# Expert stage of a mixture-of-experts block: another order of casts, token turns and comparisons

## What is computed

```
scores = softmax(xf @ router_w + router_b)
G, idx = top_k(scores.T, 512)                # 8 experts, 512 tokens each
toks = xf[idx]
h1 = relu(einsum('ekh,ehf->ekf', toks, w1) + b1)      # 256 -> 1024
eo = einsum('ekf,efh->ekh', h1, w2) + b2              # 1024 -> 256
y = zeros_like(xf).at[idx].add(eo * G)
x = x + gb * y
```

## Time and profile before

| | us |
|---|---|
| median of 3 runs | 1748.44 (1747.86 to 1748.75) |
| the profiled execution's own time | 1750.26 |
| its span in the profile | 1748.4 |
| PE busy in the span | 1678.7 |
| DVE busy | 1516.8 |
| ACT busy | 1286.0 |
| POOL busy | 232.6 |

### The profile page before, as it was taken

The page is one execution under the profiler, slowest core; times in us unless marked ns, Lnnn a source line. Parts: engine busy times, 40 slices in busy tenths (PEclk is TensorE's granted clock), DMA queues, the critical chain, the costliest instruction groups (busy, mean ns, idle before and its releaser), DMA issues. The chain is left out here.

```text
span 1748.4 us, 42933 instructions
## 1 busy us (share of the span) xinstructions
PE 1678.7 (96%) x16853; PEld 949.0 (54%) x16853; DVE 1516.8 (87%) x1956; ACT 1286.0 (74%) x2425; POOL 232.6 (13%) x300
## 2 busy tenths in 40 slices
PE   7999999999999999999999999999999997499997
PEld 4645555555555555555555555555555585277776
DVE  5578999999999999999999999999999386677873
ACT  2326888888888888888888888888888824266561
POOL 0422012100010000001000000100000012134453
PEclk9999999999999999999999999999999995599999
DMA  8660343222222233223222223332220332244532
GB/s 276 190 175 26 88 102 51 42 41 39 53 53 39 40 53 52 42 41 64 42 39 39 41 53 52 60 48 40 42 39 12 109 116 60 85 109 104 138 67 30
DMA packets 95719, 121.99 MB, mean 70 GB/s; under 512 B 26124, under 2 KB 72780, under 8 KB 92412
## 3 DMA queue, kind: packets, MB, share of 16 engines
q1 hardware_dynamic: 86556, 109.23, 28.0%
q0 software_dynamic: 6144, 8.39, 2.9%
q10 hardware_dynamic: 2816, 1.61, 0.3%
HBM read 79.36 MB, written 38.54 MB: 67 GB/s over the span
## 5 line engine op out<-in xcount | busy, mean ns | idle before, releaser
L229 DVE TENSOR_REDUCE pmax<-ps 128x2 f32<-128x1024 f32 x1024 | 1192.6, 1215 | 55.9 <-PE ps L222 49.0
L1060 ACT ACTIVATE pt<-ps 128x512 f32<-128x512 f32 x2048 | 1078.6, 600 | 182.8 <-PE ps L577 164.8
L222 PE MATMUL ps<-kp,qp 48*128 48x512 f32 x2048 | 625.4, 460 | 2.4 <-DVE pmax L229 2.4
L1119 PE MATMUL ps<-pt,v_st 128*32 128x256 f32 (+1 forms) x10752 | 589.7, 335 | 0.7 <-ACT pt L1060 0.7
L577 PE MATMUL ps<-qp,kp 50*128 50x512 f32 x2048 | 563.5, 423 | 0.7 <-ACT pt L1060 0.5
L577 PEld LDWEIGHTS ps<-qp,kp 50*128 50x128 f32 x2048 | 294.4, 185 | 265.1 <-ACT pt L1060 261.2
L1119 PEld LDWEIGHTS ps<-pt,v_st 128*32 128x32 f32 x10752 | 266.0, 109 | 261.1 <-issue 187.5
L222 PEld LDWEIGHTS ps<-kp,qp 48*128 48x128 f32 x2048 | 246.5, 184 | 107.7 <-issue 90.1
L212 POOL CAST m_parts<-rowmax_t 128x32 fp32r<-128x32 f32 x64 | 13.4, 210 | 865.6 <-DVE rowmax_t L246 865.6
L1501 POOL DMA_INDIRECT y<-contrib,scatter_at x32 | 64.7, 2023 | 98.4 <-DVE contrib L1630 80.6
L439 ACT ACTIVATE pt<-ps,xb 128x512 fp32r<-128x512 f32 x32 | 22.0, 687 | 62.2 <-PE ps L602 62.2
(11 more groups left out here) (223 smaller groups left out, 1114.9 us busy)
## 6 DMA issues: line engine op xcount, KB each, us to landing
kp<-k_parts SPq DMA_DIRECT2D x186, 128.0 KB, 4.5
v_all<-L_ffn_w SPq DMA_DIRECT2D x16, 1024.0 KB, 5.5
qp<-q_parts SPq DMA_DIRECT2D x186, 64.0 KB, 4.1
q_parts<-pt SPq DMA_DIRECT2D x16, 512.0 KB, 2.9
k_parts<-pt SPq DMA_DIRECT2D x16, 512.0 KB, 3.3
o_rows<-o_sb SPq DMA_DIRECT2D x64, 128.0 KB, 3.3
sums_c<-o_rows SPq DMA_DIRECT2D x512, 0.5 KB
m_rows<-m_parts SPq DMA_DIRECT2D x256, 2.0 KB
```

The lines of the kernel that those rows point to most:

```text
L222: last = nc.tensor.matmul(slot[:, half * CH:(half + 1) * CH], qp[rows, r, a * P:(a + 1) * P], kp[rows, r, c * CH:(c + 1) * CH], start=True ...
L229: v.reduce_max(pmax[:, u % 2, 2 * k:2 * k + 2], slot.rearrange("p (f t) -> p f t", f=2), AX.X).then_inc(groups_out, 1)
L1060: nc.scalar.activation(pt[:, s % PTS, half * CH:(half + 1) * CH], bank(n % SCORE_BANKS), ACT.Exp, scale=SCALE).then_inc(scores_out, 1)
L1119: last = mm(acc[32 * j:32 * (j + 1), first * QB:(first + many) * QB], v_st[:, h % NBUF, kt, :], probs[:, :, j * QB:(j + 1) * QB], start=kt ...
```

## The change

Four edits, all in the stage of the experts:

1. ACT reads a first-layer bank once, into `hid_f`, and the semaphore `hid_out` is raised by that. The upper piece `hid_h` is cast later from `hid_f` in SBUF, in a new function `take_hidden_high`, called for tile `f - 1` after the read of tile `f`, and for the last tile after the loop. A new semaphore `hid_high` tells DVE when it may make `hid_l`. The last expert stays as it was.
2. ACT copies the list out after tile 5 and not after tile 4.
3. A comparison step of DVE is made of eight instructions of 128 x 128, one for each tile of tokens, with that tile's column of `lane` as a scalar for each partition, and no longer of one instruction of 128 x 1024. For that, `lane` is stored in 32 bits.
4. PE turns the next tokens after tile 5 of the second half and not after tile 3.

```diff
-            lane = sb2("lane", [P, E, NT], BF16)
+            lane = sb2("lane", [P, E, NT])
...
-                        nc.scalar.activation(hid_f[f % HID_BUFS], bank(2 + f % 2), ACT.Relu, bias=bias)
-                        nc.scalar.activation(hid_h[:, f, :], bank(2 + f % 2), ACT.Relu, bias=bias).then_inc(hid_out, 1)
+                        nc.scalar.activation(hid_f[f % HID_BUFS], bank(2 + f % 2), ACT.Relu, bias=bias).then_inc(hid_out, 1)
+
+                    def take_hidden_high(e, f):
+                        act.wait_ge(hid_out, e * NF + f + 3)
+                        nc.scalar.copy(hid_h[:, f, :], hid_f[f % HID_BUFS]).then_inc(hid_high, 1)
...
                         for f in range(NF):
                             take_hidden(e, f)
-                            if f == 4 and e < last_e:
+                            if f > 0 and e < last_e:
+                                take_hidden_high(e, f - 1)
+                            if f == 5 and e < last_e:
                                 take_list(e + 1)
                         if e == last_e:
                             break
+                        take_hidden_high(e, NF - 1)
                         take_w2_high(e, 1)
...
                     def make_one_hot(n, g8):
                         dve.wait_ge(listed, n * 4 + (g8 + 1))
-                        v.tensor_tensor(one_hot[:, g8 % 2], lane[:, n, g8 * 8:(g8 + 1) * 8].unsqueeze(2).broadcast_to([P, 8, P]),
-                                        col_row[:].unsqueeze(1).broadcast_to([P, 8, P]), ALU.is_equal).then_inc(hot, 1)
+                        for t in range(8):
+                            last = v.tensor_scalar(one_hot[:, g8 % 2, t, :], col_row[:], lane[:, n, g8 * 8 + t:g8 * 8 + t + 1],
+                                                   None, ALU.is_equal)
+                        last.then_inc(hot, 1)
...
                     def take_hidden_low(e, f):
-                        dve.wait_ge(hid_out, e * NF + f + 3)
+                        dve.wait_ge(hid_high, e * NF + f + 1)
...
-                            if d == 1 and f == 3:
+                            if d == 1 and f == 5:
                                 turn_tokens(e + 1)
```

More of the change, by code:

```diff
@@ L1463, in adaln_moe_block @@
             tok_turned, tok_out, hid_full, hid_out = sem("tok_turned"), sem("tok_out"), sem("hid_full"), sem("hid_out")
-            tok_high, hid_low, w2_high, w2_low = sem("tok_high"), sem("hid_low"), sem("w2_high"), sem("w2_low")
+            tok_high, w2_high, w2_low = sem("tok_high"), sem("w2_high"), sem("w2_low")
+            hid_high, hid_low = sem("hid_high"), sem("hid_low")
             yt_full, yt_out, y_turned = sem("yt_full"), sem("yt_out"), sem("y_turned")
```

## The result

The changed kernel takes 1752.81 us (median of 9 runs), the kernel before 1748.44 (median of 9): a ratio of 1.0024, with an interval of 1.0015 to 1.0033. It is slower, by 4.4 us. One of the nine runs of the changed kernel, at 1787.62, fell into a slower state of the chip and is left out of the ratio. The prediction said 1752.1 and gave "slower" 0.55.

What follows compares the result with a forecast made beforehand. Turns were taken to be set mainly by w2's load, in a loop through PE, ACT and DVE, with PE nearly the bound. Terms +0.6, +1.2, +1.8, +1.3 and -1.2 gave +3.7 on 1748.44: 1752.1 us, range 1746.5 to 1759.5.

Steps and rivals of the forecast that it cites:

- the fourth step: DVE's fourth comparison step in an expert: 1.2 us early before, now late, so PE waits 0.7 for it.
- the list: ACT's list copy, now behind tile 5's read and a cast: PE waits 0.45 us for it in an expert.
- The chosen rate of four: DVE's 128 x 128 comparisons move data at four times the slow rate: 0.16 us each, 1.28 a step.
- four steps ahead of the first list: DVE's four comparison steps before the first list, all on the path, each 0.14 us longer: +0.6.
- expert 0 to 1: Gap between the first two turns: between 0.88 us (casts and list) and 1.35 (later gathers) longer, taken as +1.2.
- five experts: The five steady experts, bound by the weights' loop at 27.5 us for 27.15: +0.36 each, +1.8 in all.
- expert 6 to 7: The last gap between turns, with no load: PE's loop takes 27.23 us for 25.93, +1.3.
- after the last turn: PE's work behind the last turn: 1.37 us less for the moved matmuls, 0.15 more for a wait, -1.2.
- The landing goes by the gathers: Rival, 25 in 100: gathered rows land by the gathers, not w2's load; five experts cost +0.1 each, sum +2.4, 1750.8 us.
- Comparisons cheap: Rival, 15 in 100: DVE's new comparisons take 0.10 us each, the fourth step is never late; -2.5, 1746.0 us.
- slower: Rival, 12 in 100: DVE's comparisons move two elements a cycle, 1.55 us a step, +11.4, 1759.8; at one element 1774.
- POOL held off by the comparisons: Rival, 8 in 100: POOL's second scatter waits for DVE's whole longer run, gathers start at T + 19.1; +8, 1756.5 us.

Runs made afterwards that it cites:

- e11: The kernel before, run once more unchanged for its gaps: 245.3 us from the expert stage's first row to the end, 27.5 from expert 0 to 1.
- e12: The changed kernel, run once more unchanged for its gaps: 251.6 us from the expert stage's first row to the end, 30.78 from expert 0 to 1.
- e6: The changed kernel with w2's load issued only after the next expert's tokens are turned: 1749.96 us, ratio 1.0011 to the kernel before.
- e10: The changed kernel with the list's copy back behind tile 4: 1752.28 us, ratio 1.0009 to the kernel before; its trace is of its fastest run.
- e1: The kernel before with only the comparisons changed (eight 128 x 128 instructions a step): 1748.98 us against 1749.81, ratio 0.9994.
- e8: The changed kernel with DVE's fourth comparison step ahead of the lower pieces of tiles 0 and 1: 1749.83 us, ratio 1.0004 to the kernel before.
- e4: The kernel before with w2's load issued only after the next expert's tokens are turned: 1740.17 us, ratio 0.9944.
- e3: The kernel before with only the turn of the tokens moved two tiles later: 1745.48 us, ratio 0.9974.
- e2: The kernel before with only the casts changed, the list's copy kept behind tile 4: 1756.48 us, ratio 1.0041.

## Why the prediction was right, and where it was not

The total was right, 1752.1 for 1752.81, and the mechanism of the five steady experts was, but one term was mis-sized threefold and the medians hide it.

**The steps of an expert held.** Comparisons start 0.163 apart (forecast 0.16), the fourth step keeps PE 0.75 (0.7), the list 0.51 (0.45), `tok_h` 0.20 (0.15), the turn 0.41 (0.3); the load is at T + 21.66 (21.6), the gathers start at T + 18.03 (17.8). The chosen rate of four, with the fixed part of 0.127 read from 256 elements, gives the 0.163 that was measured; no run shows rate and fixed part one by one. The Trainium skill (VectorE: DVE Perf Modes, the errata section) would have made it 94 ns; this trace does not agree with its fixed 58 cycles, but agrees with its remark that many small tiles pay per tile: eight comparisons take 1.30 start to start, the one instruction that they replace 1.14.

**Each term against what the traces show** (after less before):

| term | forecast | traces |
|---|---|---|
| four steps ahead of the first list | +0.6 | +0.57 |
| expert 0 to 1 | +1.2 | +3.56 |
| five experts | +1.8 | +2.21 |
| expert 6 to 7 | +1.3 | +1.30 |
| after the last turn | -1.2 | -1.49 |
| sum | +3.7 | +6.15 |

**The step that failed is "expert 0 to 1: +1.2".** It was put between 0.88 (casts and list) and 1.35 (later gathers), and is 3.56 in the first pair and 3.3 in the second (e11 and e12). POOL's timeline in expert 0, before and then after, shows where most of it lies:

```profile
1536.96 0.94 POOL L1491 DMA_INDIRECT stage_a<-h_rows,gather_at  x1 [20.04 <-DVE gather_at L1603]
...
1539.46 0.97 POOL L1491 DMA_INDIRECT stage_a<-h_rows,gather_at  x1 [0.30 <-issue]
1540.74 1.17 POOL L1491 DMA_INDIRECT stage_a<-h_rows,gather_at  x1 [0.30 <-issue]
```

```profile
1536.41 0.94 POOL L1492 DMA_INDIRECT stage_a<-h_rows,gather_at  x1 [22.08 <-DVE gather_at L1612]
1537.66 1.24 POOL L1492 DMA_INDIRECT stage_a<-h_rows,gather_at  x1 [0.30 <-issue]
1539.20 1.63 POOL L1492 DMA_INDIRECT stage_a<-h_rows,gather_at  x1 [0.30 <-issue]
1541.14 0.95 POOL L1492 DMA_INDIRECT stage_a<-h_rows,gather_at  x1 [0.30 <-issue]
```

From the turn of expert 0, the first gather starts at 17.35 before and 19.48 after: +2.13. The second and third then take 1.24 and 1.63, beside `hid_l` and `w2_l` of DVE, and the fourth starts at 24.21 for 21.13: +3.08. The turn of expert 1 follows it by 6.27 for 5.79: +0.48. Together that is the 3.56, where the later gathers had been given 1.35 at most. The load of `w2`, by which the forecast counted, is issued 23.11 after the turn for 21.51, only +1.60.

Part of the later gathers is the clock. The windows of before, then of after, around its return:

```profile
1524.00:1526.00 2.00, 2.00 (x7) 1.52 (x6) 1.93 (x4) 0.23 (x1) 0.00 (x0) 0.51 0.00 0
```

```profile
1524.00:1526.00 2.00, 2.00 (x13) 1.10 (x13) 2.00 (x14) 0.40 (x1) 0.00 (x0) 0.65 0.00 0
```

It returns to 2.4 GHz at 1525.97 and 1525.38, that is 6.4 and 8.5 after the turn, and PE comes to the first list sum at 7.63 and 8.57: 0.94 later. The edits need not be the cause of this part: over the 14 traces the return comes 6.3 to 9.0 after the turn, at 6.3 in e6 and e10, which have the casts and the turn of the changed kernel, and at 8.2 in e1, which has neither.

The landing is the open part. Seen from the load, the turn is 7.37 behind it (1540.04) and was 5.41. Of the seven traces with the casts and the load in its old place six have 7.4 to 7.9 here, and e10 has 6.2; those without the casts and with the turn in its old place have 5.4 to 5.7. Seen from the last gather the two groups lie closer, 6.3 to 6.8 (e10 5.1) and 5.8 to 6.0, since in the first the last gather is 1.1 behind the load and in the second 0.4 ahead of it. With the load out of the way (e6) the gap is 27.79; the last gather is issued at 23.34 for 24.21 there, 0.9 of the 2.7 gained, and the rest is the landing, so the load beside the gathers costs here too. But why the rows land 1.5 later behind load and last gather than in the later experts of the changed kernel, which have the same 1.1 between the two, is not settled. In its trace all but three of the packets of the last two gathers have ended 5.5 after the load, and the last three end at 7.0. A fetch of code of 16 KB begins 0.1 to 0.7 behind the load in six traces with casts, and ahead of it in those without; but in e8 it begins 0.25 ahead, and the turn is at its latest, 7.90, so the order of the two does not go with the landing. No run moved the fetch.

**What the median shows of it.** 4.4 us, with an interval that ends at 5.8, is less than the traces' 6.2. Short falls of the clock ahead of the stage are worth up to 4 us in a single execution. In the first pair they set the changed kernel off better by 3.25, and in the second pair worse, by 0.7 (the stage begins at 1503.39 and 1504.07). How often they come in each kernel I cannot tell from medians, so part of the near hit is luck: the sum was 2.4 too low, and the medians took back 1.8.

**The rivals.** *The landing goes by the gathers* falls for the steady experts: e1 has the last gather ahead of the load and the turn still 5.6 after the load, and e4 without the load never waits for rows from expert 1 on. e3 adds what the prediction lacked: once the load is early, the turn follows the last gather, by 3.6 to 3.75. In expert 0 it is the other way round: there the later gathers are most of the loss. *Comparisons cheap* and *slower* fall by 0.163. *POOL held off by the comparisons* falls the other way: the second scatter got shorter, 2.38 for 3.94. The rows fit this: before, it ended 1.44 behind a run of comparisons and lower pieces; now it ends at 1615.05, 1.45 behind the first two lower pieces (1613.60), and the new comparisons that DVE runs in those 1.45 do not hold it up.

**By parts.** The late turn alone wins (e3, -4.3), the comparisons alone are worth nothing that can be told (e1), the casts alone cost the most (e2, some 7): 0.43 an expert on the way to the load, and the first expert. Together they cost more than e1 and e3 let hope, as the late turn uses up the 1.2 us by which the comparisons of before were early, of which e1 has 0.4 left (e8 gives that back).

## What to carry to other kernels

When an engine waits for gathered rows, look at what else is issued within a few us of the gathers: here a load of 1 MB, not needed for another expert, set the landing, and one wait that moved it behind the turn won 9.6 us (0.9944), more than every reordering of the engines' work. Two edits that remove the same wait don't add, and a later start of a consumer uses up the slack of every other producer: list how early each one is before moving it. The first turn of a loop wants its own sum, since clock, queues and head start differ there, and a total that fits says little about its terms.

## What the hardware did that I had not expected

- **POOL's indirect DMAs wait for DVE instructions with two SBUF inputs.** A scatter of 1.55 takes 3.94 behind a run of comparisons and lower pieces, and it ends 1.44 after DVE's first pause; with `tensor_scalar` comparisons in between it takes 2.38. In the kernel before a gather of 0.94 takes 1.14 beside `w2_l`, and its end comes 0.8 after that instruction's. The Trainium skill (SBUF — State Buffer, who interferes with whom) says that such an instruction contends with GpSimd's reads, and the trace agrees. It also infers that descriptors are still written beside a `tensor_tensor`; the rows show the whole instruction held up, but not whether by reading its offsets or by writing descriptors.
- **A small `tensor_scalar` with a scalar per partition has a fixed part of about 0.13 us** between starts (an estimate: 0.163 at 128 elements of bf16, less 0.033 for the data if they move at four times the slow rate of 0.133), while a single one lasts 0.25. All 256 of them have a mean of 276 ns each:

```profile
L1603 DVE TENSOR_SCALAR stage_b<-col_row,lane 128x128 bf16<-128x128 bf16 x256 | 44.5, 276 | 0.3
```

- **Short stretches of 3.4 or 6.8 us at 1.2 GHz** while PE is at work (13.16 of 15 us busy in the first window shown), in some executions and not in others of the same kernel. Traces with such a stretch ahead of the stage begin it later, between 1502.4 and 1504.4 for 1500.3 to 1501.6.
